# An attention scorer on one core: layer 3 moved within the tensor engine's hand-written order

## The reference

```python
B, S, D = (512, 200, 64); POS_DIM = 2; H1, H2 = (80, 40)
tgt = concat([target_emb over S, pos_emb over B]) @ proj_w + proj_b
din = concat([tgt, seq, tgt - seq, tgt * seq], axis=-1)
h = sigmoid(din @ w1 + b1)          # 256 -> 80
h = sigmoid(h @ w2 + b2)            # 80 -> 40
score = (h @ w3 + b3)[..., 0]       # 40 -> 1
score = where(mask == 0, -1e9, score)
attn = softmax(score, axis=-1)
out = einsum('bs,bsd->bd', attn, seq)
```

## Time and profile before

| | us |
|---|---|
| median of 3 runs | 289.61 (289.15 to 290.76) |
| the profiled execution | 288.42 |
| its span, first to last instruction | 286.3 |
| mean granted TensorE clock over the span | 0.968 of full speed |

### The profile page before, as it was taken

How to read it: one execution, slowest core, us unless ns; L and a number is a source line. 1 busy time by engine, 2 the same in 40 slices (tenths; PEclk the granted TensorE clock), 3 DMA queues, 4 the chain that set the end, 5 groups by cost and what they waited for, 6 DMA issues and landing times.

```text
span 286.3 us, 5499 instructions
## 1 busy us (share of the span) xinstructions
PE 253.4 (89%) x2084; PEld 75.2 (26%) x2084; DVE 237.9 (83%) x331; ACT 151.9 (53%) x257; POOL 193.7 (68%) x125
## 2 busy tenths in 40 slices
PE   4658999999999999999999999999999999987200
PEld 1313332232322322323223223222232232222000
DVE  3499999797897997988979979879799799549596
ACT  2003378556664675566647655756486558556200
POOL 2000000059989799799898997998979979976650
PEclk9997999999999999999999999999999999999955
DMA  7989999999999999999999999899999962503100
GB/s 120 171 123 184 172 166 252 226 150 335 161 230 263 174 319 151 155 328 154 238 254 184 326 169 203 258 177 237 238 173 331 176 243 60 235 0 96 51 0 18
DMA packets 216749, 53.68 MB, mean 187 GB/s; under 512 B 209556, under 2 KB 210068, under 8 KB 216724
## 3 DMA queue, kind: packets, MB, share of 16 engines
q1 hardware_dynamic: 211640, 52.70, 83.5%
q10 hardware_dynamic: 5084, 0.64, 1.5%
HBM read 53.20 MB, written 0.13 MB: 186 GB/s over the span
## 4 chain that ended last, share of the span: by engine, by line
PE 84%; DVE 9%; SPq 2%; DMA 1%; ACT 1%; issue 1%; DVEq 0%; ACTq 0%
PE pA L389 31%; PE pL L415 16%; PE pB L399 16%; PE pL L422 9%; PE pB L435 8%; DVE mix_v L637 3%; PE pB L445 3%; DVE pA L644 2%; DVE X L541 1%; DMA proj_b<-in_L_rec_proj_b 1%; SPq L210 1%; SPq L221 1%; DVE X L550 1%; ACT G L286 1%; DVE HidA L676 0%
## 5 line engine op out<-in xcount | busy, mean ns | idle before, releaser
L519 POOL TENSOR_TENSOR mix<-mix 128x260 f32<-128x260 f32 (+5 forms) x51 | 96.9, 1900 | 5.2 <-POOL acc L512 0.5
L286 ACT ACTIVATE G<-pL,bias 128x512 f32<-128x512 f32 x100 | 60.6, 688 | 70.4 <-PE pL L422 70.4
L277 ACT ACTIVATE HidA<-HidA,VA 128x512 f32<-128x512 f32 x100 | 67.0, 725 | 34.0 <-DVE HidA L676 34.0
L676 DVE TENSOR_TENSOR HidA<-pA,UA 128x1024 f32<-128x1024 f32 x50 | 60.7, 1213 | 24.1 <-PE pA L389 23.3
L508 POOL TENSOR_TENSOR mix<-seq_sb,E 128x4096 f32<-128x4096 f32 (+3 forms) x13 | 77.2, 5940 | 4.9 <-ACT E L314 4.6
L550 DVE SCALAR_TENSOR_TENSOR X<-pT,P_pair,X 128x512 f32<-128x512 f32 x100 | 69.9, 739 | 0.2
L541 DVE STREAM_TRANSPOSE X<-squares 128x1024 f32<-128x1024 f32 x50 | 61.7, 1234 | 0.0
L389 PE MATMUL pA<-X,w_seq 64*64 64x512 f32 x400 | 55.1, 621 | 4.2 <-DVE HidA L676 3.7
L389 PE MATMUL pA<-X,w_sb 64*64 64x512 f32 x400 | 53.5, 606 | 0.0
L506 POOL MEMSET masked<- 128x64 f32 x11 | 1.7, 151 | 71.2 <-ACT E L314 71.2
L415 PE MATMUL pL<-HidA,w2A 64*64 64x512 f32 x400 | 48.6, 601 | 0.0
(11 more groups left out here) (90 smaller groups left out, 108.2 us busy)
## 6 DMA issues: line engine op xcount, KB each, us to landing
squares<-in_L_rec_sequence_emb SPq DMA_DIRECT2D x98, 256.0 KB, 4.7
seq_sb<-in_L_rec_sequence_emb SPq DMA_DIRECT2D x12, 2048.0 KB, 9.3
seq_sb<-in_L_rec_sequence_emb SPq DMA_DIRECT2D x1, 1024.0 KB, 5.2
squares<-in_L_rec_sequence_emb ACTq DMA_DIRECT2D x2, 256.0 KB, 6.3
mask_i<-in_r_mask SPq DMA_DIRECT2D x1, 400.0 KB, 5.2
tgt_sb<-in_L_rec_target_emb SPq DMA_DIRECT2D x1, 128.0 KB, 2.2
out_dram<-result SPq DMA_DIRECT2D x1, 128.0 KB, 2.0
w_sb<-in_L_rec_w ACTq DMA_DIRECT2D x1, 80.0 KB, 3.1
```

Source lines behind the costliest of these rows:

```text
L277: last = nc.scalar.activation(h, h, ACT.Tanh, scale=0.5, bias=VA[:, 4 * u + i:4 * u + i + 1])
L286: nc.scalar.activation(G[p % NG][:, :], pL2[p % 4][:, :], ACT.Tanh, scale=0.5, bias=bias2[:, 0:1])\
L519: nc.gpsimd.tensor_tensor(mix[:, 0:k, 0:n, :], mix[:, 0:k, 0:n, :], mix[:, 0:k, n:2 * n, :], ALU.add)\
L676: nc.vector.tensor_tensor(HidA[u % NZA][:, :, :], pA[:, :].rearrange("p (i b) -> p i b", i=2), UA[:, :].unsqueeze(1).to_broadcast([P, 2, 5 ...
```

## The change

Layer 3's call moves within PE's pass: from in front of layer 2's first part to behind the second quad's layer 1 (in pass 0: behind the set-up of layer 2), in front of layer 2's last part. Nothing else is touched; ACT, DVE, POOL and SP keep their orders.

```diff
                 c = block_of_last_group(n - ST_LAG)
                 if c is not None:
                     transpose_scores(c, min(n, NGRP))
-                c = block_of_last_group(n - L3_LAG)
-                if c is not None:
-                    layer3(c, min(n, NGRP))
                 g = n - L2_LAG
                 if 0 <= g < NGRP:
                     layer2_first(g)
                 if n < NGRP:
                     layer1_first(2 * n + 1)
                 if n == 0:
                     setup_layer2()
+                c = block_of_last_group(n - L3_LAG)
+                if c is not None:
+                    layer3(c, min(n, NGRP))
                 if 0 <= g < NGRP:
                     layer2_last(g)
```

## The result

The changed kernel takes 286.95 us (median of 15 runs) against 289.61 (15 runs): 0.9931 of the time before, 95% interval 0.9905 to 0.9957, so 0.7% faster. Nine of its fifteen runs lie at 286.45 to 286.96 us and six at 289.17 to 289.53; the profiled one, 289.53 with a span of 287.5, is among the six, so its span is *longer* than the 286.3 before, and the trace has to be read stretch by stretch.

What follows compares the result with a forecast made beforehand. The order of PE's own work was taken to bound the loop. Eleven odd passes save 1.76 us and the tail costs 0.25, so -1.51 us: 288.1 us for a median of 289.61, range 287.2 to 289.9.

Steps and rivals of the forecast that it cites:

- An odd pass: PE's odd passes 3 to 23: layer 2's first part falls from 1.88 to 1.72 us, eleven times, 1.76 us less.
- The unseen change into L422: Layer 2's last part, now behind layer 3's 128x32 tiles instead of 64x64: still 1.07 us.
- The rule of the Trainium skill: Leaving 128-row tiles before layer 2's last part costs 0.027 us more, 0.3 us in all; shares the dearer change's chance, 0.17.
- The covers: Four waits in PE's loop get less cover (second quad, DVE's entry, scores copy, layer 2's first part): cost nothing.
- its reserve: Before layer 1's last part: scores copy releases the load at 0.83 us, due at 1.00 after layer 3; reserve 0.17.
- where it was said to: DVE in odd passes: 1.76 us idle before the second quad's addition goes and reappears before its next L683.
- The tail: Pass 25: layer 2's first part now leads and waits for ACT's tanh; cost 0.08 to 0.32 us, 0.25 taken.
- the sum: Whole kernel: -1.76 us in the loop plus 0.25 in the tail, -1.51 us, median 288.1 us.
- loads change nothing: SP's queue waits for DVE's transposes, which never waited for a load; a pass 0.16 us shorter changes nothing there.

Runs made afterwards that it cites:

- The halves: Changed kernel with layer 3 cut in two in odd passes up to 23, half before layer 2's first part, half before its last part: 292.38 us, 1.0075.
- the middle place: Changed kernel with layer 3 moved between layer 2's first part and layer 1's second quad: 289.38 us, 0.9999 of the kernel before.
- the experiment in front of layer 1's last part: Changed kernel with layer 3 moved behind layer 2's last part, directly before layer 1's last part: 299.03 us, 1.0312 of the kernel before.
- the two kernels with added matmuls: Changed kernel and kernel before, each with four unread matmuls added in pass 0 and three before the last layer 3: 289.64 and 288.06 us.
- the last experiment's kernel: Changed kernel with the old order in pass 25 and three added matmuls before the last layer 3: 287.95 us, 0.9938 of the kernel before.

## Why the prediction was right

*An odd pass: right.* 10.09 us for 10.25, eleven times, -1.76 us; all in the change of cut that L415 no longer pays. The halves (+3.28) and the middle place (+1.76) show that it is the count of changes and not the earlier layer 2. One reading of the rows was off without a consequence: what the earlier trace rows call passes 5 and 6 are passes 7 and 8, and what the earlier trace rows and the prediction call pass 5 at 83.90 is pass 7, since pass 3 begins at 45.37 and a pair takes 19.23 us; the pairs in the loop are alike.

*The unseen change into L422: right at 1.07.* The equal prices by the cut that is entered hold for the combination too. The rule of the Trainium skill that the prediction weighed against this (TensorE: Matmul & The Clock Gate, Step-by-step: what each phase is for: the last column has to travel down all rows of the array; by the prediction's estimate 0.027 us more behind 128-row tiles) isn't seen: 1.07 behind L435 and behind L389.

What the price is made of was not tried by a run of its own. The traces point at the weight load of the cut that is entered. In front of another cut it starts, by the profile's modelled ends, only 0.07 us before its piece (L435 at 52.42 for 52.49, L422 at 54.28 for 54.35 in the changed kernel), so little of it is hidden. In the profile of the kernel before one load lasts 109 ns for 32 columns (L399), 132 for 64 (L415) and 183 for 128 (L422), and the three prices, 0.13, 0.16 and 0.21 us, are each 0.02 to 0.03 us above. Two statements of the Trainium skill bear on this. TensorEngine Tiling (Array Packing), Tiling Modes, says that a change of tiling mode drains the engine; the late start of the loads fits that. TensorE: Matmul & The Clock Gate, LDWEIGHTS (loading the stationary operand), says that a weight load goes by its columns, at 1.2 columns per ns, an estimate of 0.027, 0.053 and 0.107 us for 32, 64 and 128 columns. The trace agrees in the steps from one to the next, 0.023 and 0.051 us, but a whole load takes some 0.08 us longer here.

*The covers: right.* The second quad's load came at 50.47, 3.29 into the pass, as in pass 2 (40.42, 3.29), without a gap. The copy of the scores ended 0.75 us after layer 3 and was released in time; its reserve, with 0.11 for the load to follow, is 55.35 - 55.21 = 0.14 us against 0.17 worked out; with the 0.76 us from layer 3's end to the load that the experiment in front of layer 1's last part showed, it would be 0.24. DVE's idle time moved to where it was said to.

*The tail: right.* +0.24 for 0.25, and gone with the old order there.

*What the sum left out.* -1.52 us is what the stretches of the change give; the medians differ by 2.66 in one comparison and 0.70 in the other. The sum went by one execution and had no term for a set-up whose pace changes from run to run (pass 0's L399: 1.85 to 3.57 us over the profiles without added matmuls). On this the two comparisons differ, not on the change: in the first, lowest and highest runs differ by 1.34 and 1.25 us, and the medians by 2.66 because that of the changed kernel lies in the lower group of its runs and that of the kernel before above its lowest ones. That a measured ratio of 0.9931 came so near the forecast 288.1 / 289.61 = 0.9948 is in part luck; the same kernel drew 0.9976 the next time. That loads change nothing was right for both traces of the first comparison, but the margin is thin: a pair of passes needs 4.19 MB, 220 GB/s at 19.07 us. From 47 to 237 us of the profiled run above 224 GB/s moved on the mean of five stretches (212 to 248); in the two kernels with added matmuls it was 216 and 213 (209 to 218), and there DVE waited. The earlier start of their loop (L422 of pass 1 at 33.07 and 33.18 us) does not by itself explain the lower pace: the kernel with layer 3 behind layer 1's last part began at 34.45, later than the 34.21 of the kernel before, and moved 216, while the last experiment's kernel began at 33.94, moved 225 and waited for nothing. All four kernels profiled on the chip of the added matmuls moved 213 to 217, all seven others with whole loads 224 to 227. Whether that belongs to the chip or only to those runs was not tried.

## What to carry to other kernels

Where PE is busy end to end, count the changes of its tile cut in the written order: matmuls of one cut placed side by side save a change each time, here 0.13 to 0.21 us, and the gain can be read from pieces that already stand so. Before moving a piece, find what it covered and what will cover its own consumer: 1.07 us of work were enough for a copy that takes 0.76 to 0.86 us with its release, none cost 0.9 us a pass. And when the bound engine gets faster, work out what the loads need per pass: 220 GB/s needed where 213 to 227 moved means that the next gain may not arrive.

## What the runs showed of the hardware

The price of a change of cut depended on the cut entered and not on the one left, in each of the orders tried: 1.85 into 128x32, 1.88 into 64x64, 1.07 into 32x128. And the row of the granted clock does not always tell the pace. Busy time by stretches in the changed kernel's profiled run:

```profile
27.21:30.71 3.50, 3.50 (x21) 0.60 (x23) 1.85 (x6) 1.05 (x2) 0.00 (x0) 1.00 1.15 181
...
267.07:269.02 1.95, 1.08 (x4) 0.71 (x4) 0.00 (x0) 0.93 (x3) 0.92 (x1) 0.50 0.00 0
```

In the second stretch the clock stands at 0.50 (the 1.2 GHz level) and the transposes take 1.10 us for 0.64. In the first L399 takes 3.50 us for 1.85 in the same pass before, as at the lower level, but the row says 1.00. In the second profile of the same kernel L399 takes 3.57 us there, and the row says 0.50. So shortly after PE has stood still the duration of a known piece is the better witness.
